# A product copied to SBUF by ScalarE before VectorE turns it by blocks, in the attention passes of block 0

## The reference, cut to what matters

```python
scores = jnp.einsum('bhnd,bhmd->bhnm', q, k) * HD ** (-0.5)
p = jax.nn.softmax(scores, axis=-1)
o = jnp.einsum('bhnm,bhmd->bhnd', p, v)
...
x = x + _attn(q, k, v) @ Wos + bos
...
x = x + _attn(h @ Wq + bq, context @ Wk + bk, context @ Wv + bv) @ Woc + boc
```

## Time and profile before

| | before |
|---|---|
| median of three runs | 3895.97 us (3895.3 to 3903.24) |
| the profiled execution, time | 3901.6 us |
| its span | 3899.6 us |
| PE busy | 3750.1 us, 96% |
| DVE busy | 2930.1 us, 75% |
| POOL busy | 2583.4 us, 66% |
| ACT busy | 1996.6 us, 51% |
| mean granted clock of PE | 0.988 |

### The profile page before, as it was taken

How to read it: one execution, slowest core, us unless ns; L and a number is a source line. 1 busy time by engine, 2 the same in 40 slices (tenths; PEclk the granted TensorE clock), 3 DMA queues, 4 the chain that set the end, 5 groups by cost and what they waited for, 6 DMA issues and landing times.

```text
span 3899.6 us, 92972 instructions
## 1 busy us (share of the span) xinstructions
PE 3750.1 (96%) x34934; PEld 3217.8 (83%) x34934; DVE 2930.1 (75%) x6035; ACT 1996.6 (51%) x6534; POOL 2583.4 (66%) x2803
## 2 busy tenths in 40 slices
PE   8999999999799999999999999899999999989999
PEld 7888877777699988888888888788888888869998
DVE  6777777777655568888888888899999898974443
ACT  4555555555433335555555555555555555553333
POOL 4666655555477767666666666677777777756776
PEclk9999999999899999999999999999999999999999
DMA  2111111111111126666666667676776767772111
GB/s 83 41 35 34 47 51 50 51 50 49 53 49 49 60 70 201 221 211 214 214 217 212 215 218 227 208 233 225 231 226 222 234 221 231 228 217 69 44 44 33
DMA packets 415197, 544.98 MB, mean 140 GB/s; under 512 B 58523, under 2 KB 311965, under 8 KB 414749
## 3 DMA queue, kind: packets, MB, share of 16 engines
q1 hardware_dynamic: 267224, 404.74, 30.7%
q10 hardware_dynamic: 147524, 134.30, 12.9%
HBM read 220.11 MB, written 184.55 MB: 104 GB/s over the span
## 4 chain that ended last, share of the span: by engine, by line
PE 79%; DVE 9%; issue 4%; POOL 3%; DMA 2%; ACT 1%; ACTq 1%; SPq 0%; DVEq 0%; POOLq 0%
PE BANKS L614 19%; PE BANKS L615 17%; PE BANKS L616 17%; PE BANKS L810 6%; PE BANKS L798 6%; PE BANKS L666 3%; PE BANKS L743 2%; PE BANKS L675 2%; POOL HL L1313 2%; PE BANKS L860 2%; PE BANKS L682 1%; DMA p_scratch<-TR 1%; DVE SN L1156 1%; DMA PB<-p_scratch 1%; PE BANKS L626 1%
## 5 line engine op out<-in xcount | busy, mean ns | idle before, releaser
L962 ACT ACTIVATE PR<-BANKS,NM 128x128 f32<-128x128 f32 x2048 | 720.9, 379 | 348.3 <-DVE NM L1142 348.0
L1301 POOL TENSOR_TENSOR PR<-PR,RL 128x512 f32<-128x512 f32 x512 | 533.0, 1041 | 335.8 <-DVE RL L1108 334.9
L614 PE MATMUL BANKS<-HH,WH 128*128 128x512 f32 x1632 | 687.8, 421 | 29.6 <-POOL HL L1313 18.7
L615 PE MATMUL BANKS<-HL,WH 128*128 128x512 f32 x1632 | 643.1, 394 | 0.0
L616 PE MATMUL BANKS<-HH,WL 128*128 128x512 f32 x1632 | 642.1, 393 | 0.0
L1313 POOL TENSOR_TENSOR HL<-HF,HH 128x512 fp32r<-128x512 f32 x192 | 256.0, 1333 | 325.3 <-DVE HH L1040 163.6
L1142 DVE TENSOR_REDUCE NM<-BANKS 128x8 f32<-128x1024 f32 x256 | 310.3, 1212 | 197.2 <-PE BANKS L810 197.1
L962 ACT ACTIVATION_READ_ACCUMULATOR PR<-BANKS,NM 128x1 f32 x2048 | 444.7, 217 | 0.0
L923 ACT ACTIVATE PT<-BANKS 128x512 f32<-128x512 f32 x512 | 278.3, 596 | 279.8 <-PE BANKS L682 279.1
L614 PEld LDWEIGHTS BANKS<-HH,WH 128*128 128x128 f32 x1632 | 309.7, 190 | 122.4 <-POOL HL L1313 24.9
L614 PE MATMUL BANKS<-WH,OH 128*128 128x256 f32 x1280 | 376.0, 294 | 30.7 <-DVE OL L1160 22.7
(11 more groups left out here) (138 smaller groups left out, 10197.1 us busy)
## 6 DMA issues: line engine op xcount, KB each, us to landing
SW<-SN SPq DMA_DIRECT2D x1024, 128.0 KB, 2.8
p_scratch<-TR SPq DMA_DIRECT2D x256, 512.0 KB, 4.7
PB<-p_scratch ACTq DMA_DIRECT2D x1024, 128.0 KB, 3.6
x_scratch<-X SPq DMA_DIRECT2D x80, 512.0 KB, 3.2
X<-x_scratch SPq DMA_DIRECT2D x80, 512.0 KB, 4.6
CX<-in_ctx SPq DMA_DIRECT2D x32, 384.0 KB, 3.4
X<-in_x SPq DMA_DIRECT2D x16, 512.0 KB, 4.4
out<-X SPq DMA_DIRECT2D x16, 512.0 KB, 2.9
```

What stands on the lines that cost most here:

```text
L614: e.matmul(o, lh, rh, start=first and i == 0, stop=False)
L615: e.matmul(o, lh, rl, start=False, stop=False)
L962: made = e.activation(pr[:, r], bank[:, r], ACT.Exp, bias=nm[:, h:h + 1], accum_out=RL[npr(t)][:, h:h + 1])
L1301: e.tensor_tensor(p3, p3, RL[npr(t)][:, :].unsqueeze(2).broadcast_to([128, 4, 128]), ALU.mult).then_inc(s_nrm, 1)
```

## The change

ScalarE gets a new stage `pv_out` at tick tb+11, behind `exp0` in its code: as soon as `pv0` is done it copies the bank, 128x512, to one new SBUF tile, OS. The transpose of `sums` on DVE waits for this copy (semaphore `s_os`) and reads OS in place of the bank. The copy waits until the transpose before has read OS (`s_to`); its wait for `s_mods` guards memory that the prologue uses. The bank is given back when the copy is done, not when the transpose is. OS lies in memory that was free in these passes. Nothing else is changed.

```diff
-                for stage, lag in (("v", -3), ("v_out", -2), ("top", 4), ("top_turn", 5), ("top_out", 5), ("pv0", 10), ("sums", 11), ("scale0", 12),
+                for stage, lag in (("v", -3), ("v_out", -2), ("top", 4), ("top_turn", 5), ("top_out", 5), ("pv0", 10), ("pv_out", 11), ("sums", 11), ("scale0", 12),
...
+            OS = sb("OS", [128, 512], stack=soft)
...
             for x in at["pv0", tick]:
-                tp.add(("pv", x), FOUR, s_to, 4 * xq(x.p, x.g) + x.b + 1)
+                tp.add(("pv", x), FOUR, s_os, 4 * xq(x.p, x.g) + x.b + 1)
...
+                for x in at["pv_out", tick]:
+                    vi = 4 * xq(x.p, x.g) + x.b
+                    q.wait_ge(s_pv0, vi + 1)
+                    q.wait_ge(s_to, vi)
+                    q.wait_ge(s_mods, 5)
+                    e.activation(OS[:, :], PS[tp.bank(("pv", x))][:, :], ACT.Copy).then_inc(s_os, 1)
...
                 for x in at["sums", tick]:
                     vi = 4 * xq(x.p, x.g) + x.b
-                    q.wait_ge(s_pv0, vi + 1)
+                    q.wait_ge(s_os, vi + 1)
                     q.wait_ge(s_no, vi - 1)
-                    e.transpose(TO[vi % 2][:, :, :, :, :].rearrange("p c e q d -> p (c e q d)"), PS[tp.bank(("pv", x))][:, :]).then_inc(s_to, 1)
+                    e.transpose(TO[vi % 2][:, :, :, :, :].rearrange("p c e q d -> p (c e q d)"), OS[:, :]).then_inc(s_to, 1)
```

More of the change, by code:

```diff
@@ L350, in build @@
         s_q, s_qb, s_k, s_kf, s_v, s_vd = (sem(k) for k in ("q", "qb", "k", "kf", "v", "vd"))
-        s_s0, s_nm0, s_toph, s_topl, s_tt, s_m, s_ts, s_to, s_rc, s_no, s_of = (
-            sem(k) for k in ("s0", "nm0", "toph", "topl", "tt", "m", "ts", "to", "rc", "no", "of"))
+        s_s0, s_nm0, s_toph, s_topl, s_tt, s_m, s_ts, s_os, s_to, s_rc, s_no, s_of = (
+            sem(k) for k in ("s0", "nm0", "toph", "topl", "tt", "m", "ts", "os", "to", "rc", "no", "of"))
         s_s, s_nm, s_exp, s_rl, s_nrm, s_pv0, s_pv = (sem(k) for k in ("s", "nm", "exp", "rl", "nrm", "pv0", "pv"))
```

## The result

| | before | after |
|---|---|---|
| median of eight runs | 3897.66 us (3893.99 to 3903.24) | 3921.44 us (3908.41 to 3936.99) |
| ratio, 95% interval | | 1.0059 (1.0043 to 1.0074) |
| the profiled execution, time | 3901.6 us | 3926.2 us |
| its span | 3899.6 us | 3924.1 us |
| ACT busy | 1996.6 us | 2063.4 us |

The change costs 24 us.

A forecast was written before the change was run, and what follows sets the result against it. PE, busy 96% of the span, was taken as the bound. From a median of 3896 us, 23 us of delay (13.4 + 8.6 + 1.0) and 2 us of clock falls gave 3921 us, range 3905 to 3942.

The forecast's parts named there:

- more falls of the clock: PE in pass 1: one or two more drops from 2.4 to 1.2 GHz, 2 us; bounds -12 and 27 us.
- Cycle A: The one of a group's four batch-element cycles where DVE's transpose precedes HH, delaying HL and PE; 0.96 us in pass 0.
- the transpose now waits for the copy: DVE's transpose waits for ACT's copy behind the exponentials: 13.4 us in pass 0, 8.6 us in pass 1.
- The transpose gets shorter: DVE's transpose reads SBUF in place of PSUM: 0.04 us less each, bounds 0 and 0.07.
- The copy: ACT gets 128 copies out of PSUM, 0.60 us each, 77 us more work on a half-idle engine, no table loads.
- Pass 1: Groups lengthen by 0.46 us at full clock (seven) and 0.60 us at half clock (nine), together 8.6 us.
- The other three cycles: In a group's other cycles DVE's idle time before NM (0.67 or 0.91 us) covers the later transpose: no cost.
- rival of the thin cover: In the other cycles 0.1 us each comes through, 10 us more, 3931 us; chance 0.08.
- absorbed delay: PE's other waits in a group shrink by what its wait for HL grows: no cost, 3896 us; chance 0.15.
- The end of pass 1: Where feed-forward starts, four more transposes lie beside PE waits of several us: 1 us, bounds 0 and 3.
- Behind it: Behind 1115 us, in the later passes without this transpose, nothing changes except the shift in time.
- rival that pass 0 would fall too: PE's clock falls in every group of passes 0 and 1: 3946 us, half of it 3933; chance 0.17.

The follow-up runs named there:

- copy_in_a: The kernel before with the copy made only for the third batch element of each group: 3929.57 us, ratio 1.0072.
- copy_not_in_a: The kernel before with the copy made only for the other three batch elements of each group, not the third: 3901.41 us, ratio 0.9999.
- second trace of the full change: The full change run again unaltered in a later job, with its own profile: 3922.12 us, ratio 1.0056.
- order_block0: The kernel before, no copy; in passes 0 and 1 only, HH goes ahead of the transpose, HF ahead of OH, the context's split ahead of HH: 3857.65 us, ratio 0.9886.

## Why the prediction was right

- **The median**, 3921 us, fell on the measured 3921.44 us. Part of that is luck: the full change's own runs lie between 3908 and 3937 us, the kernel before came out 1.7 us slower than the 3896 that I started from, and the 2 us put down for more falls of the clock weren't seen. The loss was forecast at 25 us and measured at 23.8.
- **Cycle A is the path** (step "the transpose now waits for the copy"): right, shown by copy_in_a and copy_not_in_a. 0.96 us were worked out for pass 0, 0.98 measured; both waits behind it took the full delay.
- **The transpose gets shorter** by 0.04 us: mis-sized. It takes 711 ns from SBUF and 717 from PSUM, 6 ns less. The row that I took, TR<-PR at 681 ns, has the same size but another arrangement of its input and its output; whether that makes it shorter wasn't tested. In this view (one line's instructions, with minimum, median and maximum in ns), before and after:

```profile
L1086 DVE STREAM_TRANSPOSE TO<-BANKS x128: 700/717/719, 64.8 to 1075.8; 128x512 f32<-128x512 f32 x128
...
L1094 DVE STREAM_TRANSPOSE TO<-OS x128: 695/711/714, 64.1 to 1097.4; 128x512 f32<-128x512 f32 x128
```

  The 65 ns estimated from the Trainium skill (VectorE: DVE Perf Modes, section on the TRN2 errata) were ten times too many here. The measurement decides.
- **The copy** was put at 0.60 us; its median is 598 ns. No load of tables came with it.
- **Pass 1**: 0.46 us for a group at full clock and 0.60 for one with a fall. Groups at full clock went from 31.88 to 32.40 us, 0.52 more; groups with a fall from 33.19 to 34.00, 0.81 more (over all of them, from 33.24 to 33.93 in the mean, 0.69 more). Both kinds were put too low. The sum was 8.6 us, the stretch gave 10.0.
- **The other three cycles at nothing**: right. copy_not_in_a costs 0 within 0.1%. The rival of the thin cover is out, and so is the absorbed delay. But the cover was used up less evenly than expected: 0.1 to 0.3 us were to be left, and 0.05 us is left in one cycle and 0.45 in the other.
- **The end of pass 1**, +1 us: it was -0.9 us. **Behind it** I expected a mere shift and found 3.0 us. The second trace of the full change has +2.5 and +1.1 us in their place, so neither is a cost that the change is shown to have. The last stretch takes 2814.6 us in copy_not_in_a and 2821.6 in copy_in_a, with the same code behind pass 1; what moves it stays open.
- **The clock.** One or two falls more were expected. Over the sixteen groups of the third stretch before has nine and after has nine; the second trace of the full change has five. The 2 us for them have nothing behind them. The rival that pass 0 would fall too is out: its groups stay at 1.00 with a wait of 1.58 us. The count changes from run to run by more than the one or two expected.
- **The range**, 3905 to 3942 us, had its ends from cases of which none came true (the delay absorbed, the falls more often). What it had to hold was the spread of single runs, which the prediction didn't name.

## What to carry to other kernels

What an instruction waits for in another engine's queue can cost more than the instruction: the copy of 0.60 us cost 0.98 us a group of pass 0, 0.57 of it the exponentials in front of it. Look which step behind the new wait is on the path, in the same queue, and move that step ahead of the wait; here this took the loss away, and it gained 0.8% on the kernel before as well. A reordering made for one stage belongs in that stage alone: the same three moves gained 1.1% in block 0 and lost 5% in all passes, where they put block 1's exponentials and copies of V behind HF.

## What the runs showed of the hardware

The full change spreads its single runs three times as wide as before: 3908 to 3937 us (8 runs) against 3894 to 3903. Its time goes with the mean granted clock. Over the twelve runs of both jobs, those at 0.990 to 0.992 took 3908 to 3917 us, those at 0.985 to 0.989 took 3922 to 3937 us. That isn't strict: the second trace has a clock of 0.988 against 0.989 and is 4.7 us shorter. A fall makes a group 1.60 us longer in after (1.31 in before), as two groups show:

```profile
712.01:746.01 34.00, 30.69 (x438) 25.67 (x438) 25.92 (x56) 19.63 (x39) 18.82 (x32) 0.95 0.16 48
914.20:946.60 32.40, 29.09 (x438) 24.31 (x438) 25.83 (x56) 19.60 (x39) 18.81 (x32) 1.00 0.17 50
```

In these traces PE's granted clock is either full or half, so from a mean of 0.992 to one of 0.987 the time at half clock grows by 2 x 0.005 x 3920 = 39 us. The work lost in it is, as an estimate, up to half of that, 20 us of the 29 us between the ends. In before, long and short groups of pass 1 mostly alternated; in the trace of after, by the starts of HL, eight long ones stand in a row (33.82 to 34.01 us), and in the second trace of the full change ten short ones do. Why the clock falls in one group and not in another of the same work wasn't tested. With PE's idle time shortened, in order_block0, no group of pass 1 had a fall.
